# Row-maximum scores of an attention kernel as pairs of 64-row matmuls, with more and smaller loads per head

## The chip, the cores and the metric

The kernel runs on one core of one Trainium2 chip. Its time is device microseconds (us) of one execution; lower is better. TensorE (PE) has two clock levels, 1.2 and 2.4 GHz; the profile prints the granted clock as a share of the upper one. VectorE is DVE, ScalarE is ACT, GpSimd is POOL, and SyncE is SP; SP does nothing here but wait and issue DMAs.

## The reference

Two blocks, each a mixer and a feed-forward part with layer norms between them. The change touches only the first mixer, an attention over 2 batches of 1,024 tokens with 16 heads of 8 numbers:

```python
q = split_heads(holo_linear(x, basis_q, phase_q, amp_q))
k = split_heads(holo_linear(x, basis_k, phase_k, amp_k))
v = split_heads(holo_linear(x, basis_v, phase_v, amp_v))
attn = jnp.einsum('bhqd,bhkd->bhqk', q, k) * scale
attn = jax.nn.softmax(attn, axis=-1)
out = jnp.einsum('bhqk,bhkd->bhqd', attn, v)
```

After it come a top-2 mixture of experts, a selective scan over 1,024 steps and a small gated network; all of that stays as it was.

## The kernel before, in words

A unit is one head of one batch; there are 32 (`UNITS`). q and k in float32 are each split into three bf16 parts, high, middle and low, which are stored to DRAM (`q_parts_d`, `k_parts_d`, `store_parts`). `load_unit` (L350) reads them back so that a buffer slot holds 72 rows: for each of the 3 x 3 combinations of a part of q and a part of k, the 8 numbers of the head. A matmul over these rows gives the exact product. There are four slots of `qbuf` and `kbuf`; the rows from 72 to 95 are zero.

Each unit's scores are computed twice. The first time, two units ahead, 128 queries stand on the partitions and 512 keys in the free axis: `s_half`, 16 matmuls of a unit over 96 rows (L1355), each read by one DVE reduce (L964) that takes the row maximum. These use a ring of three PSUM banks (`ring_bank`); `ring_full` counts the matmuls and `ring_read` the reads. The bank of an item is its place within the unit modulo 3, so that the first matmul of a unit waits until all of the unit before has been read. POOL splits the 1,024 maxima into three bf16 parts (`split_max`, L519 to L523), PE turns them (`max_T`, L1361, at `T_AT`, the item 4 of a pass), DVE copies the result (L961), and SP writes it into rows 96 to 98 of the slot by one small DMA (`load_max`, L356). Only then can the second computation of that unit start: `st_half`, the transposed scores less the maximum, 99 rows, 16 matmuls (L1365), which ACT turns into exponentials (L706) for the value products (L1444, eight entries of 32 columns in two groups for a pair of key tiles).

PE's program for unit u goes through eight key tiles j. For each it issues a score matmul and a transposed-score matmul in turn, twice; after every odd j come the value products of two key tiles. At j = 6 the transposed scores change to unit u + 1, and PE waits there for that unit's `load_max`. SP's program for unit u is, in this order: `load_unit(u + 3)`, `load_max` for unit u + 1, and then `store_head(u)`, four stores of the head's output, which wait for ACT's copy (L721) after the unit's last value product. POOL's program before the units is a list of memsets, iotas and selects for constants used by later parts; SP also waits for them (`constants_ready`) before it fills two DRAM arrays with zeros.

Of the kernel before, what the change touches and what calls it, by code (L numbers as in the profile page):

```python
# [9 lines left out]
BF16 = mybir.dt.bfloat16  # L10
# [13 lines left out]
ROWS = 9 * HD  # L24
KT = L // P
SCALE = HD ** -0.5
EPS = 1e-5
# [26 lines left out]
ITEMS, T_AT = 17, 4  # L54
# [23 lines left out]
def build(nc, a, out):  # L78
    ctx = ExitStack()
    with ctx:  # L80
# [11 lines left out]
        ring_bank, pv_bank, st_pair = bank[0:3], bank[3], pair[2:4]  # L92
# [45 lines left out]
        vtok = ar(NT * HEADS * HD).rearrange("p (b h k d) -> p b h k d", b=B, h=HEADS, k=KT)  # L138
        qbuf = ar(4 * L // 2).bitcast(BF16).rearrange("p (s n) -> p s n", s=4)
        kbuf = ar(4 * L // 2).bitcast(BF16).rearrange("p (s n) -> p s n", s=4)  # L140
        probs = ar(NPROB * L).rearrange("p (s n) -> p s n", s=NPROB)
        vst = ar(2 * KT * 32).rearrange("p (s k m) -> p s k m", s=2, k=KT)
        pvs = ar(2 * CH).rearrange("p (s n) -> p s n", s=2)
# [141 lines left out]
        def _(sp):  # L285
# [189 lines left out]
            def twist(i, c):  # L475
                for dst, src in ((0, 64), (32, 96), (64, 0), (96, 32)):
                    sp.dma_start(tw_in[dst:dst + 32, c, :], xT[src:src + 32, c * CH:(c + 1) * CH])\  # L477
                        .then_inc(s_(f"twisted{c}"), 16)

            with sp.Fori(0, CYCLES) as i:  # L480
                for c in range(NCH):
# [10 lines left out]
        def _(pool):  # L492
# [85 lines left out]
            def unit(i, s, last):  # L578
                u = 4 * i + s
                if not (last and s == 3):  # L580
                    pool.wait_ge(s_("probs_free"), NPROB + KT * u)
                    stage_v(u + 1, (s + 1) % 2).then_inc(s_("v_staged"), 1)
                if not (last and s > 1):
                    pool.wait_ge(s_("ring_full"), MAXT_READ + ITEMS * u)
                    split_max(u + 2, s % 2, At(base + 8 + 4 * u))

            with pool.Fori(0, UNITS // 4 - 1) as i:
                for s in range(4):
                    unit(i, s, False)
# [321 lines left out]
        def _(dve):  # L911
# [42 lines left out]

            def reduce_pass(v_unit, mslot, item0, maxT_slot):

                k = 0
                for n in range(16):
                    if n == T_AT and maxT_slot is not None:
                        dve.wait_ge(s_("ring_full"), item0 + k + 1)  # L960
                        v.tensor_copy(mT[0:24, maxT_slot, :], ring_bank[k % 3][0:24, 0:P]).then_inc(s_("ring_read"), 1)  # L961
                        k += 1
                    dve.wait_ge(s_("ring_full"), item0 + k + 1)
                    v.reduce_max(mx[:, mslot, n // 2, n % 2:n % 2 + 1], ring_bank[k % 3], AX).then_inc(s_("ring_read"), 1)  # L964
                    k += 1
                if not isinstance(v_unit, int) or v_unit >= 2:
                    dve.wait_ge(s_("max_split"), v_unit - 1)
                dve.wait_ge(s_("ring_read"), item0 + k)
                v.tensor_tensor(rowmax[:, mslot, :], mx[:, mslot, :, 0], mx[:, mslot, :, 1], ALU.max)\  # L969
                    .then_inc(s_("max_ready"), 1)  # L970

# [35 lines left out]
                else:  # L1007
                    project(0, bank[0:2])

            with dve.Fori(0, UNITS // 4 - 1) as i:  # L1010
# [255 lines left out]
            def cycle(i, first):  # L1266

                for c in range(NCH):
                    dve.wait_ge(s_(f"twisted{c}"), 64 * (i + 1))
# [33 lines left out]
        def _(pe):  # L1303
# [38 lines left out]
            pe.wait_ge(s_("resid_done"), 8)  # L1342
            pe.wait_ge(s_("v_copied"), 4)

            def ring_wait(item0, k):

                if isinstance(item0, int) and item0 == 0:
                    if k >= 3:
                        pe.wait_ge(s_("ring_read"), k - 2)
                else:  # L1350
                    pe.wait_ge(s_("ring_read"), item0 + (k - 2 if k >= 3 else 0))

            def s_half(slot, n, item0, k):
                ring_wait(item0, k)
                t.matmul(ring_bank[k % 3], qbuf[0:96, slot, (n // 2) * P:(n // 2 + 1) * P],  # L1355
                         kbuf[0:96, slot, (n % 2) * CH:(n % 2 + 1) * CH], start=True, stop=True).then_inc(s_("ring_full"), 1)

            def max_T(m, mslot, item0, k):
                pe.wait_ge(s_("max_split"), m + 1)
                ring_wait(item0, k)  # L1360
                t.matmul(ring_bank[k % 3][0:24, 0:P], mparts[:, mslot, :], ident_b[:], start=True, stop=True)\  # L1361
# [6 lines left out]
            def score_pass(v, slot, item0, maxT_slot):  # L1368

                k = 0  # L1370
                pe.wait_ge(s_(f"unit_loaded{slot}"), 32)
                for n in range(16):
                    if n == T_AT and maxT_slot is not None:
                        max_T(v - 1, maxT_slot, item0, k)
                        k += 1
                    s_half(slot, n, item0, k)
                    k += 1

            pe.wait_ge(s_("qk_cleared"), 1)
            score_pass(0, 0, 0, None)  # L1380
# [25 lines left out]

            def unit(i, s, last):
                u = 4 * i + s
                item0 = 33 + ITEMS * u
                v_slot, u1_slot = (s + 2) % 4, (s + 1) % 4  # L1410
                scores = not (last and s >= 2)
                if scores:
                    pe.wait_ge(s_(f"unit_loaded{v_slot}"), 32 * (i + (1 if s < 2 else 2)))
                k = 0
                for j in range(KT):
                    for h in range(2):
                        n = 2 * j + h
                        if n == T_AT and not (last and s == 3):
                            max_T(u + 1, (s + 1) % 2, item0, k)
                            k += 1  # L1420
                        if scores:
                            s_half(v_slot, n, item0, k)
                            k += 1
                        if last and s == 3 and j >= KT - 2:
                            continue

                        if h == 0:
                            if j == KT - 2:
                                pe.wait_ge(s_(f"max_loaded{u1_slot}"), 16 * (i + (1 if s < 3 else 2)) + 16)
                            pe.wait_ge(s_("exp_done"), KT * u + j + 1)  # L1430
                        ins = st_half(s if j < KT - 2 else u1_slot, (j + 2) % KT, h)
                        if h == 1:
                            ins.then_inc(s_("st_done"), 1)
                    if j % 2 == 0:
                        continue

# [13 lines left out]
                    if last and s == 3 and j in (1, 3):  # L1450
                        project(j // 2, bank[j // 2])

            with pe.Fori(0, UNITS // 4 - 1) as i:
                for s in range(4):
                    unit(i, s, False)
            for s in range(4):
                unit(UNITS // 4 - 1, s, True)


            def x1_T(c):  # L1460
# [292 lines left out]
```

## Time and profile before

| what | value |
|---|---|
| median of 3 runs | 1026.22 us (1024.8 to 1027.46) |
| the profiled execution | 1022.1 us, span of its trace 1020.3 us |
| mean granted PE clock | 0.885 |
| PE, DVE, ACT, POOL busy | 780.4, 764.6, 471.1, 332.0 us |
| the 32 units of attention | from about 72 to 446 us of the span |

Busy time is a sum over stages with different limits, so it does not say what ends a unit. The chain that ended last says that, and the times at which SP and POOL issue their work say what a step that is added there would push back.

### The profile page before, as it was taken

The page shows a single profiled execution, that of the slowest core. Times are in us where ns is not written, and L with a number is a line of the kernel's source. Part 1 is how long each engine was busy: PE and PEld are TensorE (multiplying, and loading weights), DVE is VectorE, ACT ScalarE, POOL GpSimd, SP SyncE. Part 2 cuts the span into 40 slices and gives each one's busy share as a digit, 9 for nine tenths or more (in the row PEclk, how much of TensorE's full clock was granted, in tenths as well). Part 3 has the DMA queues.
Part 4 walks back from the last instruction along what each step waited for, and adds up shares of the span by engine and source line. Part 5 has one row for each costly group of instructions (what it writes and reads, how often), then busy time and mean ns, then how long its engine had stood idle before and what let it go on. Part 6 is the DMA issues. An engine that isn't in the chain of part 4 may idle for free.

```text
span 1020.3 us, 12949 instructions
## 1 busy us (share of the span) xinstructions
PE 780.4 (76%) x3564; PEld 332.6 (33%) x3564; DVE 764.6 (75%) x1205; ACT 471.1 (46%) x546; POOL 332.0 (33%) x384
## 2 busy tenths in 40 slices
PE   2599999999999999886938993580767667678572
PEld 1313233233222323226526772230322222224221
DVE  5688888888888888645501122778999999998758
ACT  1416776777767677561402321584332323331442
POOL 9500000010000001001661443107977777660000
PEclk7759999999999999896878997685898989899776
DMA  4262111111111111211112333012553434420131
GB/s 118 81 231 64 36 34 31 29 30 32 35 31 34 29 29 31 63 39 59 37 57 76 117 103 102 7 35 93 185 184 127 165 132 157 144 103 1 42 80 44
DMA packets 50469, 77.19 MB, mean 76 GB/s; under 512 B 10419, under 2 KB 29286, under 8 KB 50438
## 3 DMA queue, kind: packets, MB, share of 16 engines
q1 hardware_dynamic: 45826, 70.93, 22.4%
q0 software_dynamic: 2304, 4.74, 1.4%
q10 hardware_dynamic: 2308, 1.15, 0.4%
q8 instruction: 14, 0.23, 0.1%
q14 instruction: 17, 0.14, 0.0%
HBM read 57.29 MB, written 16.16 MB: 72 GB/s over the span
## 4 chain that ended last, share of the span: by engine, by line
PE 38%; DVE 26%; issue 14%; DMA 13%; POOL 4%; ACT 3%; SPq 2%; DVEq 0%; ACTq 0%; POOLq 0%
DMA arena<-arena 9%; PE pair L1355 9%; PE pair L1444 8%; PE pair L1365 8%; DVE arena L1225 7%; DVE arena L1219 5%; PE pair L1536 4%; PE pair L1547 4%; POOL slot_x_d L604 3%; DVE arena L964 3%; DVE xnum L278 1%; SPq L477 1%; DVE ln_stats L266 1%; DVE arena L951 1%; PE pair L1596 1%
## 5 line engine op out<-in xcount | busy, mean ns | idle before, releaser
L964 DVE TENSOR_REDUCE arena<-pair 128x1 f32<-128x512 f32 x512 | 319.8, 683 | 47.1 <-PE pair L1355 45.8
L706 ACT ACTIVATE arena<-pair 128x1024 f32<-128x1024 f32 x256 | 248.3, 1021 | 137.7 <-PE pair L1365 137.7
L1355 PE MATMUL pair<-arena 96*128 96x512 bf16 x512 | 202.8, 399 | 5.6 <-DMA arena<-k_parts_d 3.8
L1365 PE MATMUL pair<-arena 99*128 99x512 bf16 x512 | 193.7, 386 | 13.8 <-DMA arena<-arena 13.5
L666 POOL TENSOR_TENSOR arena<-arena 128x1024 f32<-128x1024 f32 x64 | 150.1, 2357 | 50.8 <-DVE arena L1219 49.5
L1219 DVE TENSOR_TENSOR_SCAN arena<-pair,arena 128x1024 f32<-128x1024 f32 x64 | 145.8, 2278 | 2.7 <-POOL arena L666 2.7
L860 ACT ACTIVATE pair<-arena,alog 128x1024 f32<-128x1024 f32 x64 | 71.5, 1118 | 149.2 <-DVE arena L1219 149.2
L1654 PE MATMUL pair<-arena,ident 128*128 128x512 f32 x256 | 129.3, 629 | 11.7 <-DVE arena L1231 11.7
L1444 PE MATMUL pair<-arena 128*32 128x512 f32 x1024 | 136.7, 606 | 0.6 <-ACT arena L706 0.6
L519 POOL TENSOR_TENSOR arena<-arena 128x8 bf16<-128x8 f32 x32 | 6.5, 203 | 335.3 <-DVE arena L969 335.3
L1645 PE MATMUL pair<-arena,sel 96*128 96x512 bf16 x128 | 41.1, 404 | 79.0 <-DVE arena L1225 70.9
L1355 PEld LDWEIGHTS pair<-arena 96*128 96x128 bf16 x512 | 50.1, 98 | 157.3 <-DVE arena L964 109.9
L1225 DVE TENSOR_TENSOR arena<-arena,pair 128x1024 f32<-128x1024 f32 x64 | 76.3, 1192 | 2.1 <-PE pair L1645 2.1
L1365 PEld LDWEIGHTS pair<-arena 99*128 99x128 bf16 x512 | 49.9, 99 | 63.4 <-ACT arena L706 17.6
L1654 PEld LDWEIGHTS pair<-arena,ident 128*128 128x128 f32 x256 | 51.4, 202 | 57.3 <-issue 35.3
L760 ACT ACTIVATE arena<-pair,biasT 128x640 f32<-128x640 f32 x32 | 25.5, 795 | 80.8 <-PE pair L1536 80.8
L607 POOL DMA_INDIRECT picked_d<-arena,back_i x40 | 38.4, 960 | 58.1 <-DVE arena L1122 42.1
L1645 PEld LDWEIGHTS pair<-arena,sel 96*128 96x128 bf16 x128 | 8.3, 101 | 132.6 <-DVE arena L1225 118.1
L1098 DVE COPY arena<-pair 128x640 f32<-128x640 f32 x8 | 6.6, 825 | 51.1 <-PE pair L1525 51.1
L1547 PE MATMUL pair<-arena 128*128 128x128 f32 x320 | 37.9, 278 | 4.0 <-ACT arena L760 4.0
L1536 PE MATMUL pair<-arena 128*128 128x320 f32 x128 | 39.4, 458 | 1.1 <-DVE arena L1098 1.1
L1444 PEld LDWEIGHTS pair<-arena 128*32 128x32 f32 x1024 | 20.2, 108 | 56.1 <-issue 44.4
(258 smaller groups left out, 836.2 us busy)
## 6 DMA issues: line engine op xcount, KB each, us to landing
arena<-b_rows_d SPq DMA_DIRECT2D x64, 512.0 KB, 3.7
arena<-q_parts_d SPq DMA_DIRECT2D x32, 144.0 KB
arena<-k_parts_d SPq DMA_DIRECT2D x32, 144.0 KB
arena<-in_L_ffn_w SPq DMA_DIRECT2D x16, 256.0 KB, 3.0
arena<-xT SPq DMA_DIRECT2D x48, 64.0 KB, 2.0
slot_x_d<-zero SPq DMA_DIRECT2D x4, 645.0 KB, 5.1
arena<-slot_x_d SPq DMA_DIRECT2D x8, 322.5 KB
head_out_d<-arena SPq DMA_DIRECT2D x126, 18.0 KB
```

The lines of the kernel that those rows point to most:

```text
L666: g.tensor_tensor(dBu[:, k % HRING, :], du[:, q, :], Bs[:, k % HRING, :], ALU.mult)\
L706: sc.activation(probs[:, kt % NPROB, :], st_pair[kt % 2][:, :], ACT.Exp, scale=SCALE)\
L860: sc.activation(dA_pair[k % 2][:, :], delta[:, q, :], ACT.Exp, scale=alog[:, q % DT, n:n + 1])\
L964: v.reduce_max(mx[:, mslot, n // 2, n % 2:n % 2 + 1], ring_bank[k % 3], AX).then_inc(s_("ring_read"), 1)
L1219: v.tensor_tensor_scan(hh[:, k % HRING, :], dA_pair[k % 2][:, :], dBu[:, k % HRING, :], 0.0, ALU.mult, ALU.add)\
L1225: v.tensor_tensor(hh[:, k % HRING, :], hh[:, k % HRING, :], c_pair[:, :], ALU.mult)\
L1355: t.matmul(ring_bank[k % 3], qbuf[0:96, slot, (n // 2) * P:(n // 2 + 1) * P], kbuf[0:96, slot, (n % 2) * CH:(n % 2 + 1) * CH], start=True, ...
L1365: return t.matmul(st_pair[kt % 2][:, h * CH:(h + 1) * CH], kbuf[0:99, slot, kt * P:(kt + 1) * P], qbuf[0:99, slot, h * CH:(h + 1) * CH], s ...
L1444: ins = t.matmul(pv_bank[32 * g:32 * g + 32, :], vst[:, s % 2, kt, :], probs[:, kt % NPROB, h * CH:(h + 1) * CH], start=kt < 2, stop=kt >= ...
L1536: last = t.matmul(pair[1 + f % 2][:, h * CH:h * CH + CAP // 2], w1r[:, s, f * P:(f + 1) * P], xeT[:, s, h * (CAP // 2):(h + 1) * (CAP // 2 ...
L1547: last = t.matmul(dst, hT[:, f, k * P:(k + 1) * P], w2r[:, s, f, :], start=f == 0, stop=f == FT - 1)
L1654: ins = t.matmul(y_pair[:, h * CH:(h + 1) * CH], ident[:], hh[:, k % HRING, h * CH:(h + 1) * CH], start=n == 0, stop=n == ST_N - 1)
```

## The change

The product of the two low parts is left out of the first computation of the scores (the row maximum only), so that it has 64 rows and not 72. The rows are put in a new order in the slots, the ninth combination last (rows 64 to 71), so that the transposed scores still have all nine. The right half of the keys gets a copy of its own in partitions 64 to 127 of two new buffers, `q2` and `k2`. `s_pair` issues two matmuls, one over rows 0 to 63 for keys 0 to 511 and one over rows 64 to 127 for keys 512 to 1,023, into two banks. Between two pairs stand four transposed-score matmuls. The bank of an item is its number over all units modulo 3. The loops of PE and DVE over the units are written out. `load_unit` is six DMAs and not two; POOL issues four more for each unit (`load_twin`), the first sixteen of them ahead of its constants.

```diff
+TOP = 8 * HD
+UNIT_LOADED, TWIN_LOADED = 6 * 16, 4 * 16
...
             def load_unit(u, slot):
 
-                for buf, parts, ap in ((qbuf, q_parts_d, [[L, 3 * HD], [0, 3], [1, L]]),
-                                       (kbuf, k_parts_d, [[0, 3], [L, 3 * HD], [1, L]])):
-                    sp.dma_start(buf[0:ROWS, slot, :], bass.AP(tensor=parts.tensor, offset=u * HD * 3 * L, ap=ap))\
-                        .then_inc(s_(f"unit_loaded{slot}"), 16)
+                for dst, parts, at, ap in (
+                        (qbuf[0:48, slot, :], q_parts_d, 0, [[L, 2 * HD], [0, 3], [1, L]]),
+                        (kbuf[0:48, slot, :], k_parts_d, 0, [[0, 2], [L, 3 * HD], [1, L]]),
+                        (qbuf[48:TOP, slot, :], q_parts_d, 2 * HD * L, [[L, HD], [0, 2], [1, L]]),
+                        (kbuf[48:TOP, slot, :], k_parts_d, 0, [[3 * L, HD], [L, 2], [1, L]]),
+                        (qbuf[TOP:ROWS, slot, :], q_parts_d, 2 * HD * L, [[L, HD], [1, L]]),
+                        (kbuf[TOP:ROWS, slot, :], k_parts_d, 2 * L, [[3 * L, HD], [1, L]])):
+                    sp.dma_start(dst, bass.AP(tensor=parts.tensor, offset=u * HD * 3 * L + at, ap=ap))\
+                        .then_inc(s_(f"loaded{slot}"), 16)
...
+            def load_twin(u, slot):
+
+                for dst, parts, at, ap in (
+                        (q2[TOP:TOP + 48, slot, :], q_parts_d, 0, [[L, 2 * HD], [0, 3], [1, L]]),
+                        (k2[TOP:TOP + 48, slot, :], k_parts_d, CH, [[0, 2], [L, 3 * HD], [1, CH]]),
+                        (q2[TOP + 48:P, slot, :], q_parts_d, 2 * HD * L, [[L, HD], [0, 2], [1, L]]),
+                        (k2[TOP + 48:P, slot, :], k_parts_d, CH, [[3 * L, HD], [L, 2], [1, CH]])):
+                    pool.dma_start(dst, bass.AP(tensor=parts.tensor, offset=u * HD * 3 * L + at, ap=ap))\
+                        .then_inc(s_(f"twin_loaded{slot}"), 16)
...
+            pool.wait_ge(s_("parts_stored0"), 4 * 16)
+            for u in range(4):
+                load_twin(u, u)
             ch(g.memset(expand[:], 1.0))
...
                     pool.wait_ge(s_("ring_full"), MAXT_READ + ITEMS * u)
                     split_max(u + 2, s % 2, At(base + 8 + 4 * u))
 
+                if not last:
+                    load_twin(u + 4, s)
...
+            def ring_wait(item):
+                if item >= 3:
+                    pe.wait_ge(s_("ring_read"), item - 2)
+
+            def s_pair(slot, qt, item):
+
+                ring_wait(item + 1)
+                t.matmul(ring_bank[item % 3], qbuf[0:TOP, slot, qt * P:(qt + 1) * P], kbuf[0:TOP, slot, 0:CH],
+                         start=True, stop=True).then_inc(s_("ring_full"), 1)
+                t.matmul(ring_bank[(item + 1) % 3], q2[TOP:P, slot, qt * P:(qt + 1) * P], k2[TOP:P, slot, :],
+                         start=True, stop=True).then_inc(s_("ring_full"), 1)
...
-            with pe.Fori(0, UNITS // 4 - 1) as i:
+            for i in range(UNITS // 4):
                 for s in range(4):
-                    unit(i, s, False)
-            for s in range(4):
-                unit(UNITS // 4 - 1, s, True)
+                    unit(i, s, i == UNITS // 4 - 1)
```

On POOL, at the end of the clears, the list of before goes from the last small memset straight to the constants:

```order
L510 MEMSET arena 128x512
L511 MEMSET arena 128x16
L527 MEMSET expand 128x1024
L528 MEMSET ones_b 128x128
L529 MEMSET zero 128x1290
```

In the changed kernel the same place reads so (four such groups of DMAs stand there, of which the first is shown):

```order
L520 MEMSET arena 128x512
L521 MEMSET arena 128x16
L534 DMA arena<-q_parts_d 48x1x1024
L534 DMA arena<-k_parts_d 48x1x512
L534 DMA arena<-q_parts_d 16x1x1024
L534 DMA arena<-k_parts_d 16x1x512
...
L550 MEMSET expand 128x1024
L551 MEMSET ones_b 128x128
```

The sixteen DMAs wait for batch 0's parts in DRAM, and the constants, `stage_v(0)` and the first `split_max` have moved behind them.

On SP, in the loop over the units, before:

```order
L350 DMA arena<-q_parts_d 72x1x1024
L350 DMA arena<-k_parts_d 72x1x1024
L355 ISA
L356 DMA arena<-arena 3x8x128
L373 REGISTER_ALU
```

And now, where L360 is `load_unit` and L366 is `load_max`:

```order
L360 DMA arena<-q_parts_d 48x1x1024
L360 DMA arena<-k_parts_d 48x1x1024
L360 ISA
L360 DMA arena<-q_parts_d 16x1x1024
L360 DMA arena<-k_parts_d 16x1x1024
L360 DMA arena<-q_parts_d 8x1024
L360 ISA
L360 DMA arena<-k_parts_d 8x1024
L365 ISA
L366 DMA arena<-arena 3x8x128
```

`load_max` has moved behind six DMAs where it stood behind two. On PE, in the third quarter of a unit's program of before, one score matmul (L1355) and one transposed score (L1365) took turns:

```order
L1355 MATMUL pair<-arena 128x512
L1430 REGISTER_ALU
L1365 MATMUL pair<-arena 128x512
L1351 REGISTER_ALU
L1355 MATMUL pair<-arena 128x512
L1365 MATMUL pair<-arena 128x512
L1351 REGISTER_ALU
L1355 MATMUL pair<-arena 128x512
```

In the changed kernel (L1376 and L1378 are the two of a pair, L1388 the transposed scores, L1467 the value products):

```order
L1376 MATMUL pair<-arena 128x512
L1378 MATMUL pair<-arena 128x512
L1388 MATMUL pair<-arena 128x512 x4
L1376 MATMUL pair<-arena 128x512
L1378 MATMUL pair<-arena 128x512
L1467 MATMUL pair<-arena 32x512 x4
```

The counts are the same; the second transposed tile of two now comes ahead of the second and third score matmul.

## Rows read from the trace of the kernel before

**Rows 1.** The page: span, and busy time by engine.

```profile
span 1020.3 us, 12949 instructions
...
PE 780.4 (76%) x3564; PEld 332.6 (33%) x3564; DVE 764.6 (75%) x1205; ACT 471.1 (46%) x546; POOL 332.0 (33%) x384
```

**Rows 2.** Busy time in 40 us: start, engines' busy us, PEclk, DMA share, GB/s.

```profile
200.00:240.00 40.00, 39.45 (x224) 12.20 (x223) 35.31 (x63) 28.57 (x32) 3.93 (x19) 1.00 0.10 30
```

**Rows 3.** ACT's copy of a head's output, one for each unit.

```profile
L721 ACT COPY arena<-pair x32: 586/586/592, 86.1 to 457.5; 128x512 f32<-128x512 f32 x32
```

**Rows 4.** Chain that ended last, one unit: start us, us, what.

```profile
204.20 0.32 PE pair L1355
...
208.99 4.22 DMA arena<-arena
...
213.33 0.39 PE pair L1365
...
215.02 1.00 PE pair L1444 x8
216.02 0.32 PE pair L1355
```

**Rows 5.** Timeline of SP's queue over that unit.

```profile
205.14 1.71 SPq L379 DMA_DIRECT2D head_out_d<-arena  x4
207.14 0.86 SPq L350 DMA_DIRECT2D arena<-q_parts_d  x1
208.11 0.73 SPq L350 DMA_DIRECT2D arena<-k_parts_d  x1
208.99 0.76 SPq L356 DMA_DIRECT2D arena<-arena  x1
```

**Rows 6.** Timeline of DVE in the same unit.

```profile
207.15 0.28 DVE L961 CAST arena<-pair 24x128 bf16<-24x128 f32 x1
...
210.29 2.48 DVE L964 TENSOR_REDUCE arena<-pair 128x1 f32<-128x512 f32 x4 [0.36 <-PE pair L1355]
```

**Rows 7.** The load of the maxima, and who waited for it.

```profile
L356 SPq DMA_DIRECT2D arena<-arena x32: 742/758/822, 65.2 to 439.8; - x32
...
  PE pair L1365: 13.5, 20
```

**Rows 8.** Timeline of POOL from the start to unit 0.

```profile
17.49 0.95 POOL L527 MEMSET expand<- 128x1024 f32 x1
...
39.70 1.04 POOL L557 TENSOR_SCALAR_AFFINE_SELECT expand<-expand 128x1024 f32<-128x1024 f32 x1
...
62.07 0.21 POOL L519 TENSOR_TENSOR arena<-arena 128x8 bf16<-128x8 f32 x1 [11.14 <-DVE arena L969]
...
63.20 0.20 POOL L523 TENSOR_TENSOR arena<-arena 128x8 bf16<-128x8 f32 x1
```

**Rows 9.** Chain that ended last, before the first unit.

```profile
41.31 3.81 DMA k_parts_d<-arena
...
46.53 4.94 DMA arena<-k_parts_d
```

**Rows 10.** Timeline of PE: the first turn of maxima.

```profile
63.99 0.27 PE L1361 MATMUL pair<-ident_b,arena 128*24 128x128 bf16 x1
```

**Rows 11.** Timeline of POOL's DMAs in the mixture of experts.

```profile
496.92 0.96 POOL L604 DMA_INDIRECT slot_x_d<-xnum,slot_i  x1 [0.30 <-issue]
498.18 0.96 POOL L604 DMA_INDIRECT slot_x_d<-xnum,slot_i  x1 [0.30 <-issue]
```

**Rows 12.** SP's stores of the q parts, by line.

```profile
L335 SPq DMA_DIRECT2D q_parts_d<-arena x6: 596/619/929, 34.5 to 52.3; - x6
```

**Rows 13.** SP's DMAs of 32 rows within SBUF, with time to landing.

```profile
L477 SPq DMA_DIRECT2D arena<-xT x48: 507/590/594, 947.0 to 993.6; - x48
...
DMA to landing us min/median/max: 1.9/2.0/2.4
```

**Rows 14.** Matmuls on four row tiles of 32 rows.

```profile
L1316 PE MATMUL pair<-wcosT,basis x8: 416/482/574, 21.2 to 21.6; 32*128 32x128 f32 x8
```

More of the change, by code:

```diff
@@ L24 @@
 ROWS = 9 * HD
+TOP = 8 * HD
+UNIT_LOADED, TWIN_LOADED = 6 * 16, 4 * 16
+ALL_UNITS = UNITS // 4 * UNIT_LOADED
 KT = L // P
@@ L140, in build @@
         kbuf = ar(4 * L // 2).bitcast(BF16).rearrange("p (s n) -> p s n", s=4)
+        q2 = ar(4 * L // 2).bitcast(BF16).rearrange("p (s n) -> p s n", s=4)
+        k2 = ar(4 * CH // 2).bitcast(BF16).rearrange("p (s n) -> p s n", s=4)
         probs = ar(NPROB * L).rearrange("p (s n) -> p s n", s=NPROB)
@@ L477, in twist @@
                     sp.dma_start(tw_in[dst:dst + 32, c, :], xT[src:src + 32, c * CH:(c + 1) * CH])\
-                        .then_inc(s_(f"twisted{c}"), 16)
+                        .then_inc(s_(f"loaded{c}"), 16)
             with sp.Fori(0, CYCLES) as i:
@@ L585, in unit @@
                     split_max(u + 2, s % 2, At(base + 8 + 4 * u))
+                if not last:
+                    load_twin(u + 4, s)
+            pool.wait_ge(s_("parts_stored1"), 4 * 16)
             with pool.Fori(0, UNITS // 4 - 1) as i:
@@ L955, in reduce_pass @@
             def reduce_pass(v_unit, mslot, item0, maxT_slot):
-                k = 0
+                item = item0
                 for n in range(16):
                     if n == T_AT and maxT_slot is not None:
[L960 to L966, printed above, removed]
+                        dve.wait_ge(s_("ring_full"), item + 1)
+                        v.tensor_copy(mT[0:24, maxT_slot, :], ring_bank[item % 3][0:24, 0:P]).then_inc(s_("ring_read"), 1)
+                        item += 1
+                    dve.wait_ge(s_("ring_full"), item + 1)
+                    v.reduce_max(mx[:, mslot, n // 2, n % 2:n % 2 + 1], ring_bank[item % 3], AX).then_inc(s_("ring_read"), 1)
+                    item += 1
+                if v_unit >= 2:
                     dve.wait_ge(s_("max_split"), v_unit - 1)
-                dve.wait_ge(s_("ring_read"), item0 + k)
+                dve.wait_ge(s_("ring_read"), item)
                 v.tensor_tensor(rowmax[:, mslot, :], mx[:, mslot, :, 0], mx[:, mslot, :, 1], ALU.max)\
@@ L1343, in _, with max_T @@
             pe.wait_ge(s_("v_copied"), 4)
[L1345 to L1358, printed above, removed]
+            def ring_wait(item):
[7 more added lines that the diff above has]
+                         start=True, stop=True).then_inc(s_("ring_full"), 1)
+            def max_T(m, mslot, item):
                 pe.wait_ge(s_("max_split"), m + 1)
-                ring_wait(item0, k)
-                t.matmul(ring_bank[k % 3][0:24, 0:P], mparts[:, mslot, :], ident_b[:], start=True, stop=True)\
+                ring_wait(item)
+                t.matmul(ring_bank[item % 3][0:24, 0:P], mparts[:, mslot, :], ident_b[:], start=True, stop=True)\
                     .then_inc(s_("ring_full"), 1)
@@ L1366, in st_half, with score_pass @@
                                 qbuf[0:99, slot, h * CH:(h + 1) * CH], start=True, stop=True)
[L1368 to L1377, printed above, removed]
+            def score_pass(v, slot, item, maxT_slot):
+                pe.wait_ge(s_(f"loaded{slot}"), UNIT_LOADED)
+                pe.wait_ge(s_(f"twin_loaded{slot}"), TWIN_LOADED)
+                for qt in range(KT):
+                    if 2 * qt == T_AT and maxT_slot is not None:
+                        max_T(v - 1, maxT_slot, item)
+                        item += 1
+                    s_pair(slot, qt, item)
+                    item += 2
             pe.wait_ge(s_("qk_cleared"), 1)
@@ L1408, in unit @@
                 u = 4 * i + s
-                item0 = 33 + ITEMS * u
+                item = 33 + ITEMS * u
                 v_slot, u1_slot = (s + 2) % 4, (s + 1) % 4
@@ L1412, in unit @@
                 if scores:
-                    pe.wait_ge(s_(f"unit_loaded{v_slot}"), 32 * (i + (1 if s < 2 else 2)))
-                k = 0
+                    pe.wait_ge(s_(f"loaded{v_slot}"), UNIT_LOADED * (i + (1 if s < 2 else 2)))
+                    pe.wait_ge(s_(f"twin_loaded{v_slot}"), TWIN_LOADED * (i + (1 if s < 2 else 2)))
                 for j in range(KT):
[L1416 to L1433, printed above, removed]
+                    if 2 * j == T_AT and not (last and s == 3):
+                        if not scores:
+                            pe.wait_ge(s_("ring_read"), item)
+                        max_T(u + 1, (s + 1) % 2, item)
+                        item += 1
+                    if scores and j % 2 == 0:
+                        s_pair(v_slot, j, item)
+                        item += 2
+                    if not (last and s == 3 and j >= KT - 2):
+                        if j == KT - 2:
+                            pe.wait_ge(s_(f"max_loaded{u1_slot}"), 16 * (i + (1 if s < 3 else 2)) + 16)
+                        pe.wait_ge(s_("exp_done"), KT * u + j + 1)
+                        for h in range(2):
+                            ins = st_half(s if j < KT - 2 else u1_slot, (j + 2) % KT, h)
+                        ins.then_inc(s_("st_done"), 1)
+                    if scores and j % 2 == 1:
+                        s_pair(v_slot, j, item)
+                        item += 2
                     if j % 2 == 0:
@@ L1451, in unit @@
                         project(j // 2, bank[j // 2])
-            with pe.Fori(0, UNITS // 4 - 1) as i:
+            for i in range(UNITS // 4):
                 for s in range(4):
-                    unit(i, s, False)
-            for s in range(4):
-                unit(UNITS // 4 - 1, s, True)
+                    unit(i, s, i == UNITS // 4 - 1)
             def x1_T(c):
```

3 lines of the change are left out of this document (1 added, 2 removed).

## The prediction

> **What bounds the kernel now.** The page comes first: PE and DVE are each busy for three quarters of the span [rows 1]. That is a mean over stages, so the next view is busy time in windows of 40 us within attention. There PE is busy for 39.45 of 40 us at full granted clock and DVE for 35.31 [rows 2]. Read alone, this says that PE sets the pace and that fewer PE microseconds make a unit shorter. The chain that ended last corrects it. A unit, from its first score matmul at 204.20 to the next unit's at 216.02, lasts 11.82 us [rows 4]; over all units the copies of head outputs give (457.5 - 86.1) / 31 = 11.98 us [rows 3]. In the middle of the unit 4.22 us of the chain are a DMA within SBUF, issued at 208.99: the load of the row maxima. PE's first transposed score of the next unit starts at 213.33 [rows 4], 0.12 us after it landed. PE is nearly busy and at the same time nearly always late for that one DMA: 20 of the 32 loads held PE up [rows 7]. DVE's reads leave gaps of 0.36 us [rows 6] and are not the pace.
>
> So I follow the unit as a loop: PE's end of a unit (T = 204.20), ACT's copy, four stores of heads on SP from 205.14 to 206.85, then the two unit loads at 207.14 and 208.11, then the load of the maxima at 208.99 [rows 5], its landing, the transposed scores at 213.33, the rest of PE's unit, 216.02. In pieces: 2.94 us from T to the first unit load (S = 207.14), 6.19 us from S to the transposed scores, 2.69 us to the end. The turned maxima had been read by DVE at 207.15 + 0.28 = 207.43 [rows 6]; from then until 208.99 the load only waited behind SP's own DMAs. What stands on SP between S and this load is on the path.
>
> **The change part by part.**
>
> *Start.* POOL runs its constants from 17.49 to 40.74 [rows 8], 23.25 us that lie entirely under the wait for the q and k parts. Batch 0's parts are in DRAM at 41.31 + 3.81 = 45.12 [rows 9]. The change makes POOL wait for exactly that, then issue 16 DMAs, and only then make the constants; the first split of maxima stands behind both. POOL's only DMAs in the trace are indirect ones, 1.26 us from one start to the next (0.96 busy, 0.30 issue) [rows 11]. I take this for the direct ones: 16 x 1.26 = 20.2 us. From below an SP DMA of the cheapest kind, 1.71 / 4 = 0.43 us [rows 5], gives 6.9; from above I take a quarter more than the row, 25 us, since these carry repeated rows. Then: 45.1 + 20.2 + 23.25 = 88.5; 0.35 for the first staging of v; 1.33 for a split, from 62.07 to 63.40 [rows 8]; 0.59 from there to the turn by PE, which is at 63.99 now [rows 8, 10]. The turn comes at 90.8, which is 26.8 us later. Nothing else can run meanwhile: PE's second score pass stops at its item 4, and the ring, DVE, ACT and the units all wait for it. The 12 scores left of that pass and unit 0 follow as before. The bounds give +13 and +32 us.
>
> *The first load of a unit* becomes six DMAs, and the first pass also needs POOL's first four, 5 us after 45.1, where the k load lands at 46.53 + 4.94 = 51.47 now [rows 9]. Up to 1 us, which vanishes under the wait above: 0 here. The low clock and the coupling of pairs in the 12 last scores: +0.5.
>
> *SP in the loop.* From S to the load of the maxima there are now 1.85 us: 0.97 for a q load and 0.88 for a k load, gaps included [rows 5]. The new 48-row loads have the same form, so 0.97 + 0.88. A start takes 0.62 us for 128 rows of the q store [rows 12], 0.59 for 32 rows [rows 13] and 0.76 for the maxima's three rows [rows 7]: it goes by form more than by rows. I take 0.9 and 0.85 for the two 16-row loads, which repeat rows too, and 0.43 each for the two plain 8-row ones, as for a head store. Sum 4.46 us, so the load of the maxima starts 2.6 us later after S. Bounds 3.6 (the 16-row ones at 0.43) and 5.1 (the 8-row ones at 0.69).
>
> *Its landing.* Today it takes 4.22 us, and part of it is the queue: a k load lands 4.94 us after its issue [rows 9], which for the one at 208.11 is 213.05, and the maxima land at 213.21. With the k load issued 3.5 us ahead and not 0.88, most of this is over. A DMA within SBUF lands after 2.0 us [rows 13]; with 0.3 for the wait and form, 2.3. The four extra DMAs of POOL for each unit and the rest of the six add traffic: 0.25, an estimate between 0 and the 1 us by which landings differ. So the transposed scores start at S + 4.46 + 2.3 + 0.25 = S + 7.0 where it is 6.19: +0.8 us. Bounds S + 5.6 (3.6 + 2.0) and S + 8.4 (5.1, and 3.3 for a landing half queued).
>
> A rule of the Trainium skill bears on this (DMA: Bandwidth & Descriptors, the section on why a DMA increments its semaphore by 16): a transfer is spread over as many engines, up to 16, as divide the outermost counts of both sides. By it the 72-row k load runs on 3 engines, and the new 48-row one on 2, 24 rows for each engine in both. The smaller load would then land no earlier, and the maxima, on the lowest three, would stay behind it until about S + 6.1 to 6.7; no row here names the engines. By it the sum is the same within 0.3 us a unit.
>
> *PE.* Eight matmuls stand between 213.33 and 215.02 [rows 4], 0.21 us each, 0.22 with the gaps. Scores of a unit take 16 such slots now; as pairs that run together, 8. Before the transposed scores at j = 6 this saving only makes PE wait longer for the DMA. Behind them it counts: today 2.69 us; then four transposed scores 0.88, one pair 0.22, value products 1.00, and 0.25, an estimate, for changes between 64-row, full and 32-column forms. Sum 2.35: -0.34 us. That row tiles run together is shown by the one place that uses them: eight entries of 416 ns and more start between 21.2 and 21.6 us [rows 14].
>
> *The ring.* The wait at a unit's first item and the register work of PE's loop go. Both lie ahead of the DMA wait: nothing. A pair now needs two of three banks, so a stall of about 0.1 us a pair is possible; also ahead of the wait. Leaving out the low x low product saves nothing by itself: matmuls over 96 and over 99 rows share the same slot of 0.21 us in the chain [rows 4]. *POOL in the loop:* 4 x 1.26 = 5 us more against about 10 us in which it waits each unit; hidden, unless a DMA costs over 2.4 us.
>
> *Sum of the loop:* 2.94 + 7.0 + 2.35 = 12.3 us where it is 11.82, +0.47 in some 30 units: +14 us.
>
> *Sum:* the profiled execution has 1022.1 us, 1.8 more than its span; + 26.8 + 0.5 + 14.1 = 1063.5. The median shown is 4.1 us above that execution, so 1068 us on the median.
>
> **The rivals.** (A) As above, 1050 to 1090: 0.55. (B) The start is late, but the maxima are not: the small loads cost 0.43 each and the landing 2.0 us, the transposed scores start at S + 6.0 or earlier, a unit takes 11.3 us, -16 us: 1026 + 27 - 16 = 1037, with 1026 to 1050 around it. For it: the landing has never been seen alone here. 0.21. (C) Faster than before: PE sets the pace after all, the maxima are there in time (S + 5.0), and a unit shrinks until DVE fills it. DVE's busy share 35.31 / 40 of 11.82 is 10.43 us; with 0.1 for the ring 10.5, so -1.3 x 30 = -39 and 1026 + 27 - 39 = 1014. It decides from where the transposed scores start at S + 5.5 or earlier. Against it: four DMAs more on SP cannot be less than 1.7 us, and S + 3.6 + 2.0 is already over that point. 0.07. The Trainium skill (TensorEngine Tiling (Array Packing), the table on theoretical speedup) gives up to 2x for contractions of 64 rows or fewer; this would be that case, 16 x 0.22 / 2 = 1.8 us of PE a unit, and the chain above speaks against it. (D) SP and the queue are worse: S + 8.4, a unit of 13.8 us, +59, 1026 + 27 + 59 = 1112; or POOL's DMAs cost 2 us each and are late. From 1090 up: 0.12. (E) The change does not do what it says: a pair runs one after the other, 0.22 us more behind the wait and +6.6 us on (A): 1074. 0.05, inside (A)'s range.
>
> **How the numbers follow.** A measurement of this kernel tells 0.3% (3 us) from nothing. Slower by over 0.3%: A, E, D and nearly all of B, 0.91. Within 0.3%: the low edge of B, 0.02. Faster: C, 0.07. The range leaves out C, the foot of B and the top of D: 1038 to 1100.
>
> **What would show it.** POOL: 16 DMAs from 45, the constants behind them, the first split near 89, and PE, DVE and ACT empty from about 63 on. SP: six loads between the head stores and the load of the maxima, with 4 to 5 us in between. PE: pairs with starts a few ns apart, a longer wait of L1388 for the DMA within SBUF, a busy share that falls well under 39 of 40 us while the unit gets longer. The forecast is wrong if units take under 11.5 us, or if POOL's 16 DMAs take under 10 us.

## The result: slower, by less than half of the forecast

The changed kernel takes 1044.38 us (median of 4 runs, 1039.96 to 1047.8), the kernel before beside it 1026.84 us. The ratio is 1.0158, with a 95% interval from 1.0128 to 1.0188: 16 us slower by the ratio, where 42 us more than the 1026.22 us of the first table were forecast. The direction was right and the time was inside the range, 6 us above its lower end, but the size was not.

The page of the changed kernel, its head:

```profile
span 1042.6 us, 12429 instructions
...
PE 746.4 (72%) x3564; PEld 302.4 (29%) x3564; DVE 762.8 (73%) x1205; ACT 469.1 (45%) x546; POOL 405.1 (39%) x512
```

PE is 34 us less busy than in [rows 1] and the span is 22.3 us longer. That is more than the 16 us by the ratio: the profiled execution of before (1022.1 us) lies 4 to 5 us under its median, that of the changed kernel (1044.29 us) on it. What follows splits up the 22.3 us, and some 5 of them are scatter that can't be put to a place. ACT's copies of the head outputs say where, since there is one at the end of each unit:

```profile
L747 ACT COPY arena<-pair x32: 586/589/592, 94.7 to 480.5; 128x512 f32<-128x512 f32 x32
```

Against 86.1 and 457.5 [rows 3] the first copy is 8.6 us late and the last one 23.0. So the start costs 8.6 us, the 31 steps from unit to unit 14.4 us (12.45 us a unit where it was 11.98), and all the rest of the kernel gives back 0.7.

**The start.** The timeline of POOL in the changed kernel:

```profile
38.84 0.77 POOL L534 DMA_DIRECT2D arena<-q_parts_d  x1 [21.30 <-DMA k_parts_d<-arena]
...
47.51 0.68 POOL L534 DMA_DIRECT2D arena<-k_parts_d  x1
48.05 1.10 POOL L550 MEMSET expand<- 128x1024 f32 x1
...
69.42 1.04 POOL L580 TENSOR_SCALAR_AFFINE_SELECT expand<-expand 128x1024 f32<-128x1024 f32 x1
...
71.97 0.20 POOL L543 TENSOR_TENSOR arena<-arena 128x8 bf16<-128x8 f32 x1
```

The constants stand behind sixteen DMAs and the first split behind both, as forecast, and PE turns the first maxima at 72.22 where it was 63.99 [rows 10]. But the forecast had 90.8. Two things are off. The sixteen DMAs take 9.2 us (0.58 us from one to the next), not 20.2. And the first of them starts at 38.84, not at 45.1: the parts of batch 0 are in DRAM 6 us earlier than before. The cause of that is on DVE. This is one of its second splits in the kernel before, beside POOL's selects, and the same in the changed kernel:

```profile
25.89 12.30 POOL L551 TENSOR_SCALAR_AFFINE_SELECT sel<-sel 96x4096 bf16<-96x4096 bf16 x3
...
31.62 2.88 DVE L951 TENSOR_TENSOR arena<-arena 128x512 bf16<-128x512 f32 x1 [0.75 <-ACT arena L695]
```

```profile
29.54 0.69 DVE L977 TENSOR_TENSOR arena<-arena 128x512 bf16<-128x512 f32 x1 [0.75 <-ACT arena L721]
```

The same instruction takes 2.88 us while the selects run and 0.69 when they don't. Of the eight of before, the first four take 2.31, 2.88, 2.88 and 1.20 us and the last four, after the selects, 0.69. POOL pays too: its three long selects take 12.30 us there and 11.77 in the changed kernel.

**A unit.** The chain that ended last in the changed kernel, from one set of transposed scores to the next unit's:

```profile
202.49 1.04 PE pair L1388 x4
203.53 0.32 PE pair L1376
...
209.61 0.99 PE pair L1467 x8
...
212.05 2.43 DMA arena<-arena
...
214.53 1.04 PE pair L1388 x4
```

And SP in the same unit:

```profile
205.75 1.75 SPq L389 DMA_DIRECT2D head_out_d<-arena  x4
207.80 0.65 SPq L360 DMA_DIRECT2D arena<-q_parts_d  x1
208.55 0.67 SPq L360 DMA_DIRECT2D arena<-k_parts_d  x1
209.41 0.72 SPq L360 DMA_DIRECT2D arena<-q_parts_d  x1
210.23 0.70 SPq L360 DMA_DIRECT2D arena<-k_parts_d  x1
211.03 0.40 SPq L360 DMA_DIRECT2D arena<-q_parts_d  x1
211.62 0.29 SPq L360 DMA_DIRECT2D arena<-k_parts_d  x1
212.05 0.82 SPq L366 DMA_DIRECT2D arena<-arena  x1
```

The unit is 12.04 us here. From the first unit load (S = 207.80) to the load of the maxima are 4.25 us, its landing takes 2.43 where it was 4.22 [rows 4], and the transposed scores start at S + 6.73. The pairs do run together; PE's timeline has them 10 ns apart:

```profile
200.66 0.39 PE L1376 MATMUL pair<-arena 64*128 64x512 bf16 x1
200.67 0.39 PE L1378 MATMUL pair<-arena 64*128 64x512 bf16 x1
202.49 1.04 PE L1388 MATMUL pair<-arena 99*128 99x512 bf16 x4 [1.44 <-DMA arena<-arena]
```

What they save ahead of the DMA is spent in waiting for it, 1.44 us here. Over all units PE waits for this load 29 times, 39.7 us together, where it was 20 times and 13.5 us [rows 7]:

```profile
  PE pair L1388: 39.7, 29
```

Three units of 13.7 to 14.1 us show one more cost. Windows with PE's busy time and granted clock:

```profile
200.00:240.00 40.00, 33.85 (x209) 8.56 (x201) 33.85 (x58) 25.83 (x30) 10.65 (x30) 1.00 0.17 46
```

```profile
236.00:246.00 10.00, 8.19 (x44) 1.72 (x43) 6.93 (x13) 6.00 (x7) 2.64 (x8) 0.83 0.11 34
```

Behind the wait of the unit at 239.22 the granted clock falls to half for some 3 us (mean 0.83 over the window), and the value products of that quarter take 1.86 us and not 0.99.

### The profile page after: what moved, and what is told of

It reads as the page before. It is cut to its first block, busy times and chain, and to the rows that moved or that the text cites. A ratio compares the mean times of both kernels' runs of the same rounds, so it can differ in the third digit from the quotient of the medians.

```text
span 1042.6 us, 12429 instructions
## 1 busy us (share of the span) xinstructions
PE 746.4 (72%) x3564; PEld 302.4 (29%) x3564; DVE 762.8 (73%) x1205; ACT 469.1 (45%) x546; POOL 405.1 (39%) x512
## 4 chain that ended last, share of the span: by engine, by line
DVE 35%; PE 30%; issue 12%; DMA 10%; POOL 7%; ACT 3%; SPq 2%; DVEq 0%; ACTq 0%; POOLq 0%
DVE arena L990 12%; PE pair L1388 8%; DMA arena<-arena 7%; DVE arena L1249 7%; PE pair L1376 5%; DVE arena L1243 5%; PE pair L1467 4%; PE pair L1557 4%; PE pair L1568 4%; POOL slot_x_d L630 3%; DVE xnum L283 1%; SPq L487 1%; DVE ln_stats L271 1%; POOL sel L574 1%; POOL arena L534 1%
## 5 line engine op out<-in xcount | busy, mean ns | idle before, releaser
L990 DVE TENSOR_REDUCE arena<-pair 128x1 f32<-128x512 f32 x512 | 327.3, 685 | 66.5 <-PE pair L1378 63.1
L1388 PE MATMUL pair<-arena 99*128 99x512 bf16 x512 | 136.4, 389 | 39.8 <-DMA arena<-arena 39.7
L1467 PE MATMUL pair<-arena 128*32 128x512 f32 x1024 | 140.5, 621 | 0.6 <-ACT arena L732 0.6
L1376 PE MATMUL pair<-arena 64*128 64x512 bf16 x256 | 104.2, 407 | 31.0 <-DVE arena L990 22.4
L1378 PE MATMUL pair<-arena 64*128 64x512 bf16 x256 | 104.2, 407 | 0.0
L1376 PEld LDWEIGHTS pair<-arena 64*128 64x128 bf16 x256 | 23.9, 93 | 185.9 <-DVE arena L990 136.4
L1388 PEld LDWEIGHTS pair<-arena 99*128 99x128 bf16 x512 | 40.1, 99 | 105.5 <-DMA arena<-arena 48.3
L534 POOL DMA_DIRECT2D arena<-q_parts_d x64 | 36.0, 563 | 34.0 <-DMA k_parts_d<-arena 21.3
L1122 DVE COPY arena<-pair 128x640 f32<-128x640 f32 x8 | 6.6, 825 | 51.5 <-PE pair L1546 51.5
L534 POOL DMA_DIRECT2D arena<-k_parts_d x64 | 39.0, 609 | 8.4 <-issue 6.9
```

The lines of the kernel that those rows point to most:

```text
L534: pool.dma_start(dst, bass.AP(tensor=parts.tensor, offset=u * HD * 3 * L + at, ap=ap))\
L1376: t.matmul(ring_bank[item % 3], qbuf[0:TOP, slot, qt * P:(qt + 1) * P], kbuf[0:TOP, slot, 0:CH], start=True, stop=True).then_inc(s_("ring_ ...
L1378: t.matmul(ring_bank[(item + 1) % 3], q2[TOP:P, slot, qt * P:(qt + 1) * P], k2[TOP:P, slot, :], start=True, stop=True).then_inc(s_("ring_f ...
L1467: ins = t.matmul(pv_bank[32 * g:32 * g + 32, :], vst[:, s % 2, kt, :], probs[:, kt % NPROB, h * CH:(h + 1) * CH], start=kt < 2, stop=kt >= ...
```

## The experiments

The theory is in two parts. Q: a unit is paced by what SP issues ahead of the load of the maxima. S: the start is paced by POOL's list ahead of the first split. The rivals: the pairs pace the loop by their need of two banks or by changes of form of the array (P), or the loads' traffic does.

### after_const_first: the constants ahead of the twin loads

```diff
-            pool.wait_ge(s_("parts_stored0"), 4 * 16)
-            for u in range(4):
-                load_twin(u, u)
             ch(g.memset(expand[:], 1.0))
...
             pool.sem_inc(s_("constants_ready"), 1)
+            pool.wait_ge(s_("parts_stored0"), 4 * 16)
+            for u in range(4):
+                load_twin(u, u)
```

> The changed kernel with POOL's 16 first twin loads behind its constants and not ahead of them. Theory S (the start costs what the constants cost, since the first split of maxima stands behind them): the first turn of maxima comes back from 72.2 to about 64 us, but the q and k parts are again in DRAM only at about 45 us, because the selects run beside DVE's splits again; about 8 us less than the changed kernel, 1036. Rival (the start is hidden, the loop makes all of the loss): within 2 us of the changed kernel, 1044.

Measured: 1041.81 us, ratio to before 1.0131 (1.0098 to 1.0163); the intervals overlap, so by itself it shows little. The traces show more: the first copy comes at 91.7 and not 94.7, and the first turn of maxima, on PE:

```profile
67.83 0.28 PE L1384 MATMUL pair<-ident_b,arena 128*24 128x128 bf16 x1 [0.15 <-POOL arena L543]
```

The turn is 4.4 us earlier, not 8. The loads of unit 0 and the pairs take the rest: POOL's first DMA is again at 45.5, the last of SP's six loads lands at 54.3 where the k load landed at 51.5 [rows 9], and at half clock a pair makes DVE wait, 1.39 us for two items where single matmuls take 1.2. S holds, with a smaller price.

### after_max_first and before_max_first: the load of the maxima first on SP

The same edit in the changed kernel and in the kernel before:

```diff
-                if not (last and s > 0):
-                    sp.wait_ge(s_("st_done"), KT * u + 1)
-                    load_unit(u + 3, (s + 3) % 4)
                 if not (last and s == 3):
                     load_max(LAST_READ if last and s == 2 else MAXT_READ + ITEMS * (u + 1), (s + 1) % 4, (s + 1) % 2)
+                if not (last and s > 0):
+                    sp.wait_ge(s_("st_done"), KT * u + 1)
+                    load_unit(u + 3, (s + 3) % 4)
```

> The changed kernel with SP's order in a unit turned round: the load of the maxima ahead of the six unit loads. Theory Q (the loop is paced by what stands on SP ahead of the load of the maxima, 4.2 us from the first unit load to it): the transposed scores no longer wait for the DMA, a unit falls from 12.4 us on average to 10.6 to 10.9, where DVE fills it; 45 us less, about 1000. Rival P (a pair of matmuls with two of three banks, or the changes of form of the array, pace the loop): a unit stays over 12 us and the time within 5 us of 1044. A third outcome: unit loads become late, a unit of 11 to 11.5, about 1015.

> The kernel before, with the load of the maxima ahead of its two unit loads on SP, and nothing else. Theory Q: the wait of 0.2 to 0.6 us a unit goes and PE's own work of 11.4 to 11.5 us paces a unit, 10 to 15 us less than before, about 1014. Rival: PE already sets the pace and the wait is only slack between it and the DMA; no change, 1026.

Measured: 1007.13 us, ratio 0.9789 (0.9756 to 0.9822), and 1015.72 us, ratio 0.9888 (0.9856 to 0.9919). Both follow Q. In the changed kernel a unit falls to 10.93 and 11.02 us in turn, a little over the 10.6 to 10.9 expected, and in the kernel before to 11.45 to 11.77. The chain of a unit in the changed kernel with this edit has no DMA left:

```profile
203.17 1.29 DVE arena L990 x2
...
204.66 2.49 DVE arena L990 x4
207.15 0.05 issue
207.20 0.39 PE pair L1376
207.58 0.00 PE pair L1378
207.59 0.97 PE pair L1388 x4
208.56 0.32 PE pair L1376
208.88 0.00 PE pair L1378
208.88 0.99 PE pair L1467 x8
```

Three quarters of a unit are PE's, 2.6 us each. In the one with the turn of the maxima the pair waits for four reduces, since the turned maxima take one of the three banks: that is what remains of P, about 0.5 us a unit.

### after_both: both edits

> Both edits together. If the two losses are apart, their gains add: 8 + 45 us less than the changed kernel, about 992, and 34 us less than the kernel before. If they overlap, the result is that of the later load order alone, about 1000.

Measured: 1002.29 us, ratio 0.975 (0.9716 to 0.9784). The gains add about as they are: 2.6 and 37.3 us apart, 42.1 us together. The expected 992 had both terms too large.

### before_six_loads: only SP's loads

The kernel before, its two unit loads replaced by the six of the changed kernel, and the waits on them from 32 to 96.

> The kernel before, with its unit load split into the six DMAs of the changed kernel (and the row order that goes with them), nothing else. Theory Q (SP's issue time ahead of the load of the maxima is on the path): from the first unit load to the transposed scores 6.7 us as in the changed kernel where it was 6.2, PE's 2.69 us behind them unchanged, a unit 0.5 us longer, 15 us in all: about 1042. Rival (the loss of the changed kernel is in its POOL loads and in PE's forms): within 3 us of before, 1027.

Measured: 1041.18 us, ratio 1.0153 (1.0123 to 1.0184): by itself this part of the change loses as much as the whole. SP and the chain in this kernel:

```profile
203.30 0.65 SPq L355 DMA_DIRECT2D arena<-q_parts_d  x1
...
207.55 0.82 SPq L361 DMA_DIRECT2D arena<-arena  x1
```

```profile
207.55 2.29 DMA arena<-arena
...
209.96 0.39 PE pair L1370
```

From the first load to the transposed scores are 6.66 us where they were 6.19, and the mean unit is (475.5 - 88.5) / 31 = 12.48 us where it was 11.98.

### after_serial and both_serial: pairs one after the other

The second matmul reads the rows of the first, so that both stand in one row tile; all loads stay.

```diff
-                t.matmul(ring_bank[(item + 1) % 3], q2[TOP:P, slot, qt * P:(qt + 1) * P], k2[TOP:P, slot, :],
+                t.matmul(ring_bank[(item + 1) % 3], qbuf[0:TOP, slot, qt * P:(qt + 1) * P], kbuf[0:TOP, slot, CH:L],
```

> The changed kernel with the second matmul of a pair taken from the same 64 rows as the first, so that the two run one after the other; all its loads stay. Theory Q (only the pair behind the DMA wait counts): 0.22 us a unit, 7 us in all, about 1051. Rival (the pairs' gain is in full in the changed kernel and something else eats it): 8 x 0.22 us a unit, 55 us, about 1100.

> The same edit in the kernel with both repairs (constants first, maxima first). There nothing hides PE: a quarter of a unit is 2.60 us with pairs and 3.04 without, so a unit of 12.2 us where it is 10.97, 37 us more: about 1039. Rival (DVE paces that loop and the pairs are worth little there too): within 5 us of 1002.

Measured: 1060.98 us, ratio 1.0358 (1.0322 to 1.0395), and 1057.76 us, ratio 1.0322 (1.0289 to 1.0354). Both are above what was expected, by 10 and 19 us. In the changed kernel the mean unit goes from 12.45 to (495.8 - 103.2) / 31 = 12.66 us, 6.8 us in all. That is Q's number, but not by Q's step. PE waits for the maxima in few units now:

```profile
  PE pair L1388: 10.0, 10
```

Most of its units last 12.29 or 12.46 us, just as in both_serial, where nothing on SP is in the way: without pairs PE's own work has become as long as SP's chain and a little longer, and the small price is the distance between the two. The other 8.5 us were in no theory: they lie between the first turn of maxima, at 72.2 in both, and the first copy. Only 1.3 of them are there by the first value products (85.94 against 84.65). The rest comes because the granted clock stays at half until about 101 us, where in the changed kernel it is full from about 86. The same window in this kernel and in the changed one:

```profile
88.00:92.00 4.00, 4.00 (x12) 0.78 (x15) 2.24 (x5) 1.94 (x2) 0.00 (x0) 0.50 0.08 27
```

```profile
88.00:92.00 4.00, 4.00 (x28) 0.92 (x27) 3.96 (x7) 3.33 (x4) 0.00 (x0) 1.00 0.07 23
```

Why it rises later there is not shown. With both repairs a unit goes from 11.20 to 12.59 us on average, 43 us by the copies where 37 were expected; 36.5 of them are in the first 27 units, of 12.3 to 12.5 us each, and the rest in the last four. The medians are 55 us apart: 4.5 us more lie ahead of the first copy, and the profiled execution of both_serial (1049.95 us) is 8 us under its median. PE's timeline there:

```profile
203.04 0.39 PE L1376 MATMUL pair<-arena 64*128 64x512 bf16 x1
203.26 0.38 PE L1378 MATMUL pair<-arena 64*128 64x512 bf16 x1
203.57 1.04 PE L1388 MATMUL pair<-arena 99*128 99x512 bf16 x4
```

A quarter is now 3.03 us, where the same number of matmuls takes 2.85 in the kernel before, whose two kinds of scores have one form. So a change of form costs about 0.1 us (the 0.31 from L1378 to L1388 against 0.22), and the pairs, which save 0.44 a quarter, give back 0.2 of it. The same pairs are thus worth 6.8 us in one kernel's loop and some 40 in another's. That most of their gain is hidden in the changed kernel is shown.

### before_const_late: the constants late, no pairs

The kernel before, with a wait for `parts_stored0` ahead of POOL's constants.

> The kernel before with POOL's constants behind the wait for batch 0's parts, as in the changed kernel, but without any twin load. Theory L (POOL's long selects and DVE's splits of q and k, which read two tensors in SBUF, keep each other out): those DVE instructions take 0.69 us each and not up to 2.88, the parts are in DRAM near 38.5 us and not at 45.1, the constants end near 61.5 and the first turn of maxima comes at about 63.5, as before: the gain and the loss cancel, 1026 within 3 us. Rival (the splits are slow for another reason, such as DMA traffic): parts at 45, constants until 68, the turn near 70: 1033.

Measured: 1025.48 us, ratio 0.9988 (0.9963 to 1.0012). All eight second splits take 0.69 us, and then PE's first turn:

```profile
31.46 0.69 DVE L952 TENSOR_TENSOR arena<-arena 128x512 bf16<-128x512 f32 x1 [0.76 <-ACT arena L696]
```

```profile
62.16 0.28 PE L1362 MATMUL pair<-ident_b,arena 128*24 128x128 bf16 x1 [2.68 <-POOL arena L523]
```

The turn is at 62.2 against 64.0 [rows 10]: 7 us gained on the splits, 5 lost on the constants. So the twin loads have no part in it. Nor have POOL's memsets and iotas: they run here from 38.16 us on, beside the last two splits, which still take 0.69. Beside the slow splits of before POOL ran nothing but selects. The same delay now strikes another DVE instruction with two inputs in SBUF, the one that joins the maxima, which takes 0.17 us elsewhere and here runs beside a select:

```profile
55.57 2.65 DVE L970 TENSOR_TENSOR arena<-arena 128x8 f32<-128x8 f32 x1
```

### after_no_loop_twins: POOL without its loads in the loop

`load_twin(u + 4, s)` left out of POOL's unit and PE's wait for it cut to the first load. The right halves of the keys are those of the first four units throughout, so that part of the row maxima is left out.

> The changed kernel without POOL's four twin loads in each unit; the right halves of the keys are then those of the first four units throughout, so the maxima are those of other heads. Theory Q (the unit is paced by SP's queue; POOL's loads are hidden and only add 0 to 0.25 us of traffic to the landing of the maxima): a unit 0 to 0.25 us shorter, 1037 to 1044. Rival (the traffic of the twin loads delays the landing by a half us or more): below 1030.

Measured: 1037.87 us, ratio 1.01 (1.0073 to 1.0127). The load of the maxima lands sooner:

```profile
211.12 2.04 DMA arena<-arena
213.16 0.05 issue
213.20 1.04 PE pair L1386 x4
```

The mean unit is (470.8 - 94.7) / 31 = 12.13 us and not 12.45: 0.32 us for traffic, 10 us in the loop by the traces and 6.5 by the medians. By the traces that is a little more than Q gave it (0 to 0.25 a unit); it is less than the rival wanted.

### selects_late and before_repaired: the best version, and what the pairs are worth in it

On SP, the load of the maxima is first and the unit loads are four units ahead; on POOL the cheap constants come first, then the twin loads, and the long selects only behind the first split:

```diff
+            pool.sem_inc(s_("zero_ready"), 1)
             ch(g.memset(carry[:], 1.0))
...
+            pool.wait_ge(s_("parts_stored0"), 4 * 16)
+            for u in range(4):
+                load_twin(u, u)
...
             split_max(0, 0, ch)
+            select_sel(0)
+            select_sel(1)
             split_max(1, 1, ch)
+            select_sel(2)
```

before_repaired has the same two repairs without the pairs, the twins, or the longer lead of the unit loads.

> A version meant to be the fastest: the load of the maxima first on SP; POOL's cheap constants under the wait for the parts, then the twin loads, and the three long selects of one constant only behind the first split of maxima, so that they run neither beside DVE's splits of q and k nor ahead of the first maxima; unit loads four units ahead and behind the load of the maxima. The parts are in DRAM at 38 us as in the changed kernel and the first turn of maxima comes near 60 us where it is 67.8 with both repairs: 7 us less, about 995. If the lock between the selects and DVE is not what made the splits slow, parts at 45 and about 1002.

> The kernel before with the two repairs that need no pairs: the load of the maxima first on SP, and the long selects behind the first split of maxima. 7 us less than with the first alone, about 1009. Against the fastest version with pairs (995.6) it tells what the pairs are worth once nothing hides them: 13 us by this. Rival (the lock gives nothing, the start is paced by the loads): 1015.

Measured: 995.56 us, ratio 0.9691 (0.9665 to 0.9717), and 1007.51 us, ratio 0.9819 (0.9743 to 0.9894). selects_late is 6.7 us faster than after_both, where 7 were expected. The splits of q and k are short a second time, in the kernel with pairs:

```profile
30.12 0.69 DVE L982 TENSOR_TENSOR arena<-arena 128x512 bf16<-128x512 f32 x1 [0.75 <-ACT arena L726]
```

Between the two stand 12 us. By ACT's copies the loop gains 13.7 us through the pairs ((432.2 - 85.6) / 31 = 11.18 us a unit against (440.1 - 79.8) / 31 = 11.62), and the start loses 5.8 (the first copy at 85.6 against 79.8); 1.6 us more come behind the last copy, and 2.4 by the distance of the profiled executions from their medians. The 12 us are uncertain by several: before_repaired has four runs, one of them at 1013.4 us, and its interval is 15 us wide. They also hold what the longer lead of the unit loads gives, which was not tried alone.

## Why the prediction was right in kind and wrong in size

*What bounds the kernel.* Right. The chain, and not PE's 39.45 busy microseconds of 40, told that SP's queue paces a unit; before_six_loads and the two kernels with the maxima first show it from both sides.

*Start.* This is the step that failed: +26.8 us forecast, +8.2 measured at the first turn of maxima (72.2 against 64.0). The structure was right and two terms were mis-sized. The price of a POOL DMA was taken from the indirect ones, 1.26 us; a direct one takes 0.58, which is 11 us for sixteen. And the starting point was taken as given, 45.1; by moving the selects the change also freed DVE's splits, and the parts were there at 38.8, which is 6.3 us. The constants took 22.4 us, not 23.25. Together 18.1 of the 18.6 us that the turn was early against the forecast. The forecast had named its own sign for this: it is wrong if units take under 11.5 us, which they did not, or if POOL's 16 DMAs take under 10 us, and they took 9.2. The row that shows this was in the trace of before: eight instructions of one form, some of 0.69 and some of 2.88 us, the long ones just beside POOL's selects. The forecast read POOL's constants as hidden and did not ask whom they held up. The Trainium skill has the rule (SBUF — State Buffer, the section on the two separate sides): a DVE instruction with two SBUF inputs and a GpSimd instruction that reads SBUF exclude each other for the whole instruction. The traces agree: L947 with one input in PSUM takes 0.68 us beside the selects, L951 with both in SBUF up to 2.88.

*First load of a unit and low clock*, +0.5: too small, hidden in the changed kernel by the wait for POOL, but visible once that is gone (after_const_first: the turn at 67.8, not 64).

*SP in the loop.* 4.46 us forecast, 4.25 measured. *Landing.* 2.3 + 0.25 forecast, 2.43 measured; without the twin loads 2.04. *The transposed scores* at S + 7.0, measured S + 6.73. *PE behind them* 2.35, measured 204.78 - 202.49 = 2.29. The unit of these timelines: 12.3 forecast, 12.04 measured. The loop's sum, +14.1 forecast, +14.4 by ACT's copies; but this agreement is partly luck. Of the first 27 units, the 24 at full clock take 12.21 us on average where it was 11.84: 0.37 us lost in each, 10 us in all, and not 0.47 and 14. The three with the clock at half, which the forecast did not have, add 5 us. The last four units together take no longer than before (51.3 us against 51.6). And with the scatter of 5 us in the profiled executions, the loop's loss is not known to better than that.

*The ring.* Called free ahead of the wait, which it was; with the wait gone it costs about 0.5 us a unit.

*The rivals.* The time, 1044.38 us, fell in the range of (B), 1026 to 1050, and not in that of (A), 1050 to 1090. What happened was not (B), though: its transposed scores at S + 6.0 or earlier would have made units shorter than before, and its start was as late as (A)'s. It was (A)'s loop with a start of a third of the forecast size. (D), with S + 8.4 or a POOL DMA of 2 us, fell. (C) fell: the change alone never came near DVE's pace, but with one reorder on SP the same pairs reach 0.979. (E) fell: the pairs run together.

## What to carry to other kernels

When an engine is busy for 39 of 40 us, look still at what ends its waits: a small DMA behind other DMAs on the same queue can pace the loop, and then a faster matmul only waits longer. Put a load that someone waits for ahead of the loads that are needed a unit later; here this reorder gives 1.1% without any pairs and turns the pairs from a loss into a gain. An engine's idle stretch is not free to fill or to empty: ask which instructions of its neighbours change in length when work is moved out of it or in.

## What the runs showed of the hardware that was not expected

- A DVE subtraction of 128 x 512 with both inputs in SBUF takes 0.69 us alone and up to 2.88 us beside POOL's selects of 3.8 to 4.1 us; the same with one input in PSUM stays at 0.68. A small one of 128 x 8 with both inputs in SBUF takes 0.17 us and 2.65 beside a select.
- A direct DMA issued by POOL takes 0.58 us from one start to the next, an indirect one 1.26.
- Two matmuls in two row tiles of 64 rows start 0 to 10 ns apart; a change from full to 64-row form, back, or from either into 32-column form costs about 0.1 us (0.31 us to the next start and not 0.22).
- In the changed kernel, with waits of 1.4 us on average in each 12 us unit, the granted clock falls to 1.2 GHz for about 3 us in three of 28 units. Of the kernels in which PE does not wait for the maxima none shows it before the last four units, but neither does after_no_loop_twins, with waits of 1.2 us. That the waits are the cause is likely, not shown.
